# Graph network, four layers with residual norms: the dense pass without rows of its second norm, and its final row operation on GpSimd

## What is computed

```python
# x: 50000 x 256, 12500 edges (src, dst)
x = _layernorm(x + _L0_gnn_ref(...))   # two dense layers with batch norm over all nodes
x = _layernorm(x + _L1_gnn_ref(...))   # attention over edges, summed by src
x = _layernorm(x + _L2_gnn_ref(...))   # attention with q, k, v over edges, summed by dst
x = _layernorm(x + _L3_gnn_ref(...))   # x @ W for every node (self loops) and edges by dst
```

## Time and profile before

| | us |
|---|---|
| median of 3 runs (4596.85 to 4601.44) | 4597.76 |
| profiled execution, own time | 4595.28 |
| profiled execution, span | 4593.2 |
| dense pass, 200 tiles | about 1762 to 2719 |
| GAT stage | about 2723 to 3375 |
| first attention pass, 100 tiles | about 3378 to 3692 |

### The profile page before, as it was taken

One profiled execution on the slowest core, in us unless ns is written; L12 is line 12 of the kernel. 1 busy time (PEld: TensorE's weight loads), 2 busy tenths in 40 slices (PEclk: granted clock), 3 DMA queues, 4 the chain that ended last, 5 costly groups with the idle time before them and its releaser, 6 DMA issues. The chain is left out here.

```text
span 4593.2 us, 91353 instructions
## 1 busy us (share of the span) xinstructions
PE 3488.3 (76%) x17524; PEld 2616.9 (57%) x17524; DVE 3319.8 (72%) x11837; ACT 2592.9 (56%) x6036; POOL 2942.8 (64%) x2825
## 2 busy tenths in 40 slices
PE   4899934446999997888888878777769958850587
PEld 2799922224888885555555645555558845530365
DVE  7788833334555567999999979888965577740798
ACT  0687712222666666777777748787854436640376
POOL 0366658885333335777777767888877836667476
PEclk9999955556999998998899877778889979985799
DMA  1688823333444447888888843333345537763344
GB/s 43 182 238 237 236 68 79 80 80 88 161 159 162 162 163 231 275 272 273 272 271 272 272 150 92 99 99 101 99 111 128 127 98 211 211 169 82 95 135 117
DMA packets 450182, 734.81 MB, mean 160 GB/s; under 512 B 171319, under 2 KB 284845, under 8 KB 450028
## 3 DMA queue, kind: packets, MB, share of 16 engines
q1 hardware_dynamic: 276204, 571.18, 40.5%
q0 software_dynamic: 173824, 162.17, 14.8%
HBM read 351.68 MB, written 389.16 MB: 161 GB/s over the span
## 5 line engine op out<-in xcount | busy, mean ns | idle before, releaser
L1222 PE MATMUL nodes_xp<-w_self,nodes_x3T 128*125 128x256 f32 x1600 | 493.6, 436 | 130.3 <-DVE nodes_elu L1333 123.5
L1080 POOL TENSOR_TENSOR mlp_r_parts<-mlp_r,mlp_r_parts 128x500 fp32r<-128x500 f32 x200 | 253.5, 1268 | 403.4 <-ACT mlp_r_parts L1066 394.2
L1371 POOL TENSOR_SCALAR nodes_x<-nodes_u,nodes_r,nodes_nm 125x256 f32<-125x256 f32 x800 | 459.8, 588 | 74.6 <-DVE nodes_nm L1326 67.8
L1222 PEld LDWEIGHTS nodes_xp<-w_self,nodes_x3T 128*125 128x125 f32 x1600 | 296.5, 206 | 208.7 <-issue 114.4
L774 PE MATMUL gram<-gin_both,gin_am 125*128 125x257 f32 x404 | 206.6, 667 | 266.2 <-DVE gin_both L757 254.0
L1379 POOL TENSOR_TENSOR nodes_v<-nodes_elu,nodes_x 125x512 f32<-125x512 f32 x200 | 253.7, 1269 | 176.6 <-DVE nodes_elu L1333 176.3
L1105 DVE BATCH_NORM_STATS2 mlp_stats<-mlp_y 128x500 f32 (+1 forms) x200 | 136.2, 681 | 255.6 <-ACT mlp_y L1056 255.6
L774 PEld LDWEIGHTS gram<-gin_both,gin_am 125*128 125x128 f32 x404 | 118.5, 323 | 354.2 <-issue 322.8
L178 POOL DMA_INDIRECT by_src<-rank_recs,rank_place x100 | 119.7, 1197 | 289.9 <-DVE rank_recs L504 289.3
L1019 PE MATMUL mlp_y<-mlp_hT,mlp_w 128*128 128x500 f32 x1200 | 296.7, 396 | 1.6 <-DVE mlp_hT L1099 0.9
L1019 PE MATMUL mlp_y<-mlp_r_parts,mlp_w 128*128 128x500 f32 x1200 | 287.4, 388 | 0.8 <-ACT mlp_y L1056 0.8
(11 more groups left out here) (406 smaller groups left out, 11561.4 us busy)
## 6 DMA issues: line engine op xcount, KB each, us to landing
X<-nodes_x SPq DMA_DIRECT2D x200, 448.0 KB
Y<-mlp_y SPq DMA_DIRECT2D x100, 500.0 KB
nodes_y<-Y SPq DMA_DIRECT2D x100, 500.0 KB
rank_xin<-x SPq DMA_DIRECT2D x100, 448.0 KB
XP<-rank_xc SPq DMA_DIRECT2D x100, 448.0 KB
mlp_h<-XP SPq DMA_DIRECT2D x100, 448.0 KB
nodes_x<-x SPq DMA_DIRECT2D x100, 448.0 KB
out<-nodes_out SPq DMA_DIRECT2D x100, 448.0 KB
```

Source lines behind the costliest of these rows:

```text
L1080: pool.tensor_tensor(rp[:, s, 1, m, :], r[:, s, m, :], rp[:, s, 0, m, :], ALU.subtract).then_inc(s_rp, 1)
L1222: pe.matmul(xp[:, b, j, :], x3T[:, s, k, P * j:P * j + P], w_self[:, k, 0:F], start=(k == 0), stop=False)
L1371: pool.tensor_scalar(dst[:, s, j, :], u[:, at.slot(LONG), j, :], r[:, s, k, j:j + 1], nm[:, s, k, j:j + 1], ALU.mult, ALU.add).then_inc(do ...
```

## The change

Rows of the second norm are no longer made by the dense pass. One table `XX` of 2N rows holds `x1` in its first half and, in its second half, the rows that the GAT stage writes (before that, the second half is used for `Y2`). A sorted edge record gets a flag: records by dst are written at their place, or `SHIFT` further on if their dst is also a src. `segments` loads both places and adds them. In the first attention pass the flag picks the half from which a dst row is gathered. Rows with flag 0 are of `x1` and get their norm there: VectorE takes moments, ScalarE makes scale and shift and writes `xn`. Rows with flag 1 get scale 1 and shift 0 by the same instructions. In the dense pass `outs` goes to GpSimd, with a new step `means2` on VectorE for its shift.

```diff
 # histogram
+            for rows in halves:
+                sp.dma_start(rows, env["zcol"][0:P, 0:120].unsqueeze(1).broadcast_to([P, 10, 120])).then_inc(s_clear, 16)
...
+            ch.step(dve.tensor_scalar(incl[:, 0, :, :], count[:, 0, :, :], 1.0, float(SHIFT), ALU.min, ALU.mult))
+            ch.step(dve.tensor_tensor(base[:, 1, :, :], base[:, 1, :, :], incl[:, 0, :, :], ALU.add))
 # segments
+            sp.dma_start(far[:, :, :], beyond).then_inc(s_dma, 16)
+            sp.dma_start(nxt_far[0:P - 1, :], beyond[1:P, 0, 0:2]).then_inc(s_dma, 16)
...
+            ch.step(dve.tensor_tensor(env["srec"][1][:, :, :], env["srec"][1][:, :, :], far[:, :, :], ALU.add))
+            ch.step(dve.tensor_tensor(nxt[:, 1, :], nxt[:, 1, :], nxt_far[:, :], ALU.add))
+            ch.step(dve.tensor_copy(env["srec"][1][:, :, 3], far[:, :, 3]))
 # nodes, SyncE
             def load(at):
                 c = at.slot(AHEAD)
-                wait(sp, s_z, at.count(4, 4 - 4 * AHEAD))
-                sp.dma_start(y[:, c, :, :].rearrange("p k n -> p (k n)"),
-                             env["Y2"][at.col, :, :].rearrange("o p n -> (o p) n")).then_inc(s_y[c], 16)
                 wait(sp, s_u, at.count(2, 2 - 2 * AHEAD))
...
+                wait(sp, s_z, at.count(4, 4 - 4 * AHEAD))
+                sp.dma_start(y[:, c, :, :].rearrange("p k n -> p (k n)"),
+                             env["Y2"][at.col, :, :].rearrange("o p n -> (o p) n")).then_inc(s_y[c], 16)
...
-                sp.wait_ge(s_x2, at.count(2 * J, 2 * J))
-                put(x2_v, at, x2, o_2)
...
-            run_stages(sp, [(11, store_out), (7, store), (0, load)], NCH, NCH, unroll=AHEAD)
+            run_stages(sp, [(12, store_out), (7, store), (0, load)], NCH, NCH, unroll=AHEAD)
 # nodes, VectorE
-            def outs(at):
-                s, c = at.slot(RING), at.slot(RING) // 2
+            @pairs_only
+            def means2(at):
+                p = both_long(at)
                 dve.wait_ge(s_r2, at.uses(PAIR, 1, 1))
-                wait(dve, o_o[c], at.uses(RING, 32))
-                for j in range(J):
-                    dve.tensor_scalar(out[:, s, j, :], v[:, s, j, :], mv2[:, s, j, 0:1], r2[:, s, j:j + 1],
-                                      ALU.subtract, ALU.mult).then_inc(s_out, 1)
+                wait(dve, s_out, at.count(J, J - J * LONG))
+                dve.scalar_tensor_tensor(out=nm2[:, p, :], in0=r2[:, p, :], scalar=-1.0, in1=mv2[:, p, :, 0],
+                                         op0=ALU.mult, op1=ALU.mult).then_inc(s_nm2, 1)
 # nodes, GpSimd
+            def outs(at):
+                s, c, l = at.slot(RING), at.slot(RING) // 2, at.slot(LONG)
+                pool.wait_ge(s_nm2, at.uses(PAIR, 1, 1))
+                wait(pool, o_o[c], at.uses(RING, 32))
+                pool.sem_inc(s_hold_p, 1)
+                for j in range(J):
+                    pool.tensor_scalar(out[:, s, j, :], v[:, l, j, :], r2[:, l, j:j + 1], nm2[:, l, j:j + 1],
+                                       ALU.mult, ALU.add).then_inc(s_out, 1)
+            run_stages(pool, [(11, add), (16, outs), (6, first)], tiles, tiles, LONG, LONG)
 # gat_edges, GpSimd
+            pool.tensor_scalar(write2[:, :], meta["write"][:, :], N, None, ALU.add).then_inc(s_index, 1)
 # attention_scores
+            pool.wait_ge(s_index, 4)
...
+            def normed(at):
+                s = at.slot(RING)
+                act.wait_ge(s_q, at.count(2, 2))
+                ch = Chain(act, ca, at.count(3))
+                ch.step(act.activation(lnq[:, s, :], q[:, s, :], ACT.Ln, bias=rec[:, at.col, 3]))
+                ch.step(act.activation(c[:, s, :], lnq[:, s, :], ACT.Exp, scale=-0.5))
+                ch.step(act.activation(nm[:, s, :], mean[:, s, :], ACT.Copy, scale=c[:, s, :]))
+                wait(act, s_t, at.count(1, 1 - RING))
+                wait(act, s_o[s], at.uses(RING, 32))
+                act.activation(xn[:, s, :], xd[:, s, :], ACT.Identity, bias=nm[:, s, :], scale=c[:, s, :]).then_inc(s_xn[s], 1)
...
-            run_stages(act, [(0, copy_rows), (1, copy_out)], T)
+            run_stages(act, [(0, normed), (1, copy_rows), (3, copy_out)], T, **stages)
...
+            def variance(at):
+                s = at.slot(RING)
+                dve.wait_ge(s_mv, at.count(1, 1))
+                wait(dve, s_xn[s], at.uses(RING))
+                dve.scalar_tensor_tensor(out=q[:, s, :], in0=mv[:, s, 1:2], scalar=EPS, in1=fresh[:, at.col],
+                                         op0=ALU.add, op1=ALU.mult).then_inc(s_q, 1)
+                dve.tensor_scalar(mean[:, s, :], mv[:, s, 0:1], unfresh[:, at.col], None, ALU.mult).then_inc(s_q, 1)
...
-            run_stages(dve, [(0, rest), (1, dots)], T)
+            run_stages(dve, [(0, stats), (3, rest), (0, aggregate), (4, dots), (0, variance)], T, **stages)
```

More of the change, by code:

```diff
@@ L49 @@
 RC = 12
+SHIFT = 1 << 14
 CUTS = ((0, 112), (112, 13))
@@ L1271, in rsqrt2 @@
             def rsqrt2(at):
-                p = both(at)
+                p = both_long(at)
                 act.wait_ge(s_q2, at.uses(PAIR, 1, 1))
-                wait(act, s_out, at.count(J, J - J * RING))
+                wait(act, s_out, at.count(J, J - J * LONG))
                 ch = Chain(act, c_rb, at.uses(PAIR, 2))
@@ L1286, in add @@
                 wait(dve, s_x1, at.count(J, J - J * LONG))
-                wait(dve, s_x2, at.count(J, J - J * LONG))
                 wait(dve, s_x3, at.count(J, J - J * LONG))
@@ L1322, in means @@
                 wait(dve, s_x1, at.count(J, J - J * RING))
-                wait(dve, s_x2, at.count(J, J - J * RING))
                 wait(dve, s_x3, at.count(J, J - J * RING))
-                for k in range(3):
+                for k in range(2):
                     dve.scalar_tensor_tensor(out=nm[:, p, k, :], in0=r[:, p, k, :], scalar=-1.0,
@@ L1358, in _ @@
-            aggregate1, aggregate2 = moments_of(st, s_st1, mv, LONG, s_mv1, mv_free), moments_of(st2, s_st2, mv2, RING, s_mv2, mv2_free)
-            run_stages(dve, [(14, outs), (2, add), (12, stats2), (10, elus), (2, stats1), (12, aggregate2), (4, means), (2, aggregate1),
+                wait(dve, s_out, at.count(J, J - J * LONG))
+                wait(dve, s_nm2, at.uses(PAIR, 1, 1 - LONG // PAIR))
+            stats1, stats2 = stats_of(u, LONG, s_u, st, s_st1, s_mv1), stats_of(v, LONG, s_v, st2, s_st2, s_mv2)
@@ L1360, in _ @@
+            aggregate1, aggregate2 = moments_of(st, s_st1, mv, LONG, s_mv1, mv_free), moments_of(st2, s_st2, mv2, LONG, s_mv2, mv2_free)
+            run_stages(dve, [(14, means2), (2, add), (12, stats2), (10, elus), (2, stats1), (12, aggregate2), (4, means), (2, aggregate1),
                              (12, variances2), (2, variances1)], tiles, tiles, LONG, LONG)
@@ L1417, in gat_edges @@
     stages, AHEAD = dict(unroll=LONG, behind=LONG), 3
+    write2, s_index = ph.sb("write2", [P, T + 1], I32), ph.sem("index")
     with nc.Block() as block:
@@ L1434, in put_x2 @@
                 pool.wait_ge(s_x2, at.count(1, 1))
-                dram.scatter(env["X2"], meta["write"][:, at.col], x2[:, s, :], s_w2[s])
+                second.scatter(env["XX"], write2[:, at.col], x2[:, s, :], s_w2[s])
             def put_xp(at):
@@ L1843, in attention_scores @@
     meta, rec = env["meta"][1], env["srec"][1]
-    xd, xs = ph.sb("xd", [P, RING, F]), ph.sb("xs", [P, RING, F])
+    LONG = 2 * RING
+    xd, xs, xn = ph.sb("xd", [P, RING, F]), ph.sb("xs", [P, LONG, F]), ph.sb("xn", [P, RING, F])
+    st, mv = ph.sb("stats", [P, RING, 6]), ph.sb("mv", [P, RING, 2])
+    q, mean, lnq, c, nm = (ph.sb(n, [P, RING, 1]) for n in ("q", "mean", "lnq", "c", "nm"))
+    fresh, unfresh = ph.sb("fresh", [P, T]), ph.sb("unfresh", [P, T])
+    dst2, src2 = ph.sb("dst2", [P, T], I32), ph.sb("src2", [P, T], I32)
+    s_index = ph.sem("index")
+    stages = dict(unroll=LONG, behind=LONG)
     xT = ph.sb("xT", [128, RING, 2, 4, P], F32R)
```

152 lines of the change are left out of this document (88 added, 64 removed).

## The result

The changed kernel takes 4577.11 us (median of 5 runs, 4575.38 to 4578.60) against 4597.76 before (5 runs, 4591.02 to 4601.44): ratio 0.9955, 95% interval 0.9941 to 0.9970, so faster by 0.3% to 0.6%. 4583 was forecast.

A forecast was written before the change was run, and what follows sets the result against it. VectorE was taken to bound the dense pass (4.706 us per tile), GpSimd the first attention pass (3.02). Terms -158, +134 and +9 sum to -15: 4597.8 to 4583 us, own range 4550 to 4615, overall range 4525 to 4650.

The forecast's parts named there:

- both large terms: Forecast time differences of two stages: -158 us for the dense pass, +134 us for the first attention pass.
- the ring: First attention pass: VectorE's and ScalarE's list order makes each iteration need `dots` in series, 4.05 us per tile over GpSimd's 3.02.
- Dense pass, VectorE at 3.70: Dense pass: VectorE's busy time falls from 4.54 to 3.70 us per tile, 3.37 plus 0.33 for disturbance by GpSimd.
- six small instructions: Dense pass, VectorE per two tiles: `means2`, two `nodes_nm`, three `nodes_q`, each 0.24 us longer beside GpSimd, 0.72 per tile.
- Coupling of 0.2: Dense pass: 0.2 us per tile added because VectorE and ScalarE wait for each other, giving 3.90.
- 200 x (3.90 - 4.706): Dense pass: 200 tiles at 3.90 us instead of 4.706, -161 us, or -158 with the later last step.
- sum of 4.05: First attention pass: intervals from `qs` around through VectorE and ScalarE back to `qs`, added to 4.05 us per tile.
- ScalarE's floor of 3.69: Dense pass: rival where tiles get down to 3.69 us, ScalarE's time without waits for VectorE; total 4525 us, chance 0.18.
- The ring does bind: First attention pass: denies the rival that waits are met ahead and only ramp is paid, total 4455 us, chance 0.08.
- The rest: Outside the two large stages: `segments`, `histogram`, `write2` and the index step before the first gather, together +9 us.
- The clock's 0.25: First attention pass: TensorE at the lower clock for 0.44 of the time raises 4.05 to 4.30 us per tile.
- The outcome to which I gave 0.19: First attention pass: rival where TensorE's clock stays low, 4.71 us per tile, total 4624 us, slower, chance 0.19.

The follow-up runs named there:

- the slow subtraction: Changed kernel with GpSimd's `first` and `outs` of the dense pass subtracting the mean, without `means2` and one `nodes_nm`: 5015.46 us, ratio 1.0915 to the kernel before.
- the three runs on it: Each against the changed kernel, first attention pass: `variance` ahead of `dots`, 4467.25 us; `att_v` before `att_qs`, 4597.05; ScalarE's and VectorE's lists written out, 4525.02.
- one half alone: Kernel before with dense-pass `outs` on GpSimd, `means2` and longer buffers, rows of the second norm still made there: 4572.08 us, ratio 0.9948.
- the other: Changed kernel with dense-pass `outs` back on VectorE, no `means2`, rows of the second norm left out: 4704.38 us, ratio 1.0246 to the kernel before.

## Why the prediction was right, point by point

The total, -15 forecast and -20 measured, is nearer than its terms deserve. The direction of each term was right, and so was the ring, but the sizes of both large terms came out by errors that cancel, which is luck. Point by point:

- *Dense pass, VectorE at 3.70.* Measured 3.74, right as a sum and wrong as a mechanism. The step behind it charged each of six small instructions 0.24, since I read in the earlier trace rows that each of the three `nodes_nm` ends with a GpSimd instruction. That row merges them: taken singly they last 0.47, 0.15 and 0.53, so the second waited for nothing even there. In the loop they stand beside the long `nodes_v`: the first waits for its end and the rest take 0.15. So leaving out one `nodes_nm` and one `nodes_q` saved 0.06 per tile and not 0.17 ((79.5 + 33.2) / 170 - (69.0 + 25.7) / 156.5), and `means2` costs 0.25 and not 0.08: 0.28 of the 0.37 by which 3.74 lies over 3.37, where I had 0.33 for six waits. The Trainium skill (SBUF — State Buffer, section "SBUF: two separate sides") calls the shared pair of ports an exclusive lock that one instruction holds to its end while the other blocks; the 78, 85 and 79 groups beside `nodes_v` agree. Other rows are less simple: with `outs` on GpSimd and the rows of the second norm kept, 46 of the 84 `nodes_nm` that took over 0.25 us outlast the ends of two or three GpSimd instructions (up to 1.85 us), and beside the slow subtraction the waits are as long as 3.97 us and often end inside a GpSimd instruction. No run here says why.
- *Coupling of 0.2.* The term was mis-sized: 3.83 - 3.74 = 0.09. What it stood for, ScalarE's 3.69, was the better figure.
- *200 x (3.90 - 4.706).* The rate of the loop was applied to all 200 tiles, but the first and last twenty or so are quicker: 199 intervals of `nodes_u` average 4.589 before and 3.777 after. So both rates were 0.12 too high, 23 to 25 us each, and the two errors cancel: -158 met -164 by luck.
- *The ring.* Right, shown by the three runs on it, and the largest step. Its sum of 4.05 was mis-sized for the loop, 4.39: `att_q` to the logarithm, reckoned 0.24 + 0.04, took 0.48, the gap behind the score 0.32 and not 0.22, the step from row operation to cast 0.51 and not 0.47. For two small instructions in a loop I chose the lower bound's neighbourhood; it was the upper.
- *Rivals.* ScalarE's floor of 3.69 was not reached as shipped (3.83), though it is next. The ring does bind.
- *The rest.* `segments` +6.4 (7 forecast). Of the 6.4, the added loads take 4.4, where I had 5: from the first issue to the first use it is 16.45 us now and was 12.05. The exchange of the loads did cost, by the trace, at the start, where no chunk lies ahead: the first `y` is asked for 1.1 us later, behind `x`, and VectorE's first add comes 3.9 us later. No run undid the exchange alone. I had named the cover and not asked where it begins. The rest as a whole is +12, not +9.

*The clock's 0.25* was wrong: the sum came to 4.30 by this term alone, and it measured nothing. That 4.30 nevertheless met the average of 4.27 is luck: the ring's sum was 0.34 too low for the loop, the clock's term filled 0.25 of that, and the first and last tiles, at 3.89 and less, pull the average under 4.39. The clock was granted at 0.96 here, but where it was low the ring turned no slower: nine times in this stage, and the `att_prod` around them follow each other after 4.38 to 4.57 us, as elsewhere. From 3506.54 to 3509.96 it stood at 0.50, the lower level:

```profile
3506.54:3509.96 3.42, 3.41 (x16) 3.41 (x17) 1.83 (x8) 1.51 (x5) 2.02 (x2) 0.50 0.35 84
```

Twelve products took 2.92 us there, and 1.70 in the tile before:

```profile
3501.70 1.70 PE L1935 MATMUL att_kq<-att_w_parts,att_xT 128*125 128x256 f32 x12 [1.55 <-DVE att_xT L2006]
...
3506.55 2.92 PE L1935 MATMUL att_kq<-att_w_parts,att_xT 128*125 128x256 f32 x12 [2.02 <-DVE att_xT L2006]
```

The `att_prod` around them start at 3503.15, 3507.54 and 3512.10. The 4.56 of the second interval is what every eighth tile takes, where the loop turns: 3542.88 to 3547.43 too, 4.55, and there the clock is at 1.00. TensorE has a pause of some 1.5 us in each tile, is not in the ring, and so has time to be slow. The outcome to which I gave 0.19 rested on an engine off the path.

## What to carry to other kernels

When work is moved into another stage, add up the resources, but then follow the lists: an engine that serves two steps of one tile in order can tie them into a ring longer than any engine's own time, and a slack engine's clock doesn't matter then. Place the small instruction that others wait for ahead of the long dependent step, and price a ring from rows of the same kind of code, looped or written out. For an engine's floor take the window less its waits, not its busy time. Before small instructions are priced from the mean of their group, look at single ones in the timeline: here one of them held the whole wait, and leaving out another saved next to nothing. Test the halves: here one half alone gave as much as the whole, and the other was worth having, beside the first, only with its order mended.

## What the hardware showed unexpectedly

- GpSimd's tensor_scalar on 125x256 took 1427 ns with (subtract, mult), 558 with (add, mult), 560 with (mult, add).
- Of two or three adjacent `nodes_nm` on 4 elements per partition, begun while GpSimd ran its `nodes_v` of 1.27 us, the first took 0.79 to 0.80 us and each other 0.15, 163 times out of 163; one of 8 elements in their place took 0.81.
- VectorE's `nodes_q` on 4 elements per partition took 188, 211, 417 or 1304 ns on average, in kernels that differ in what GpSimd runs.
- The same ring of instructions on VectorE and ScalarE turned in 3.89 us written out and in 4.39 in a loop.
